# Decoder layer on one core: q and k transposed by DMA as fp16 halves, rotary sums on GpSimd, all engine orders laid out anew over eight stages

## What is computed

```python
x = x + attn(layernorm(x), wq, wk, wv, wo)      # causal, 8 heads of 128
x = x + xattn(layernorm(x), ctx, ctx)           # gelu(h @ ctx.T) @ ctx, 375 rows
x = x + ffn(layernorm(x), w1, b1, w2, b2)       # quantised to 8 bit, relu, 1024 hidden

# attn:
q, k = rope(rmsnorm(x @ wq)), rope(rmsnorm(x @ wk)); v = x @ wv
s = (q * mult) @ (k * mult).T - 1e30 * later
o = softmax(s) @ v;  return o @ wo
```

## Time and profile before

| | us |
|---|---|
| median of three runs | 731.2 (730.33 to 732.17) |
| the profiled execution | 730.79 |
| its span in the trace | 729.1 |
| one batch in the middle of the run | 21.39 |
| granted TensorE clock, mean | 0.986 |

### The profile page before, as it was taken

The page is one execution under the profiler, slowest core; times in us unless marked ns, Lnnn a source line. Parts: engine busy times, 40 slices in busy tenths (PEclk is TensorE's granted clock), DMA queues, the critical chain, the costliest instruction groups (busy, mean ns, idle before and its releaser), DMA issues.

```text
span 729.1 us, 15114 instructions
## 1 busy us (share of the span) xinstructions
PE 697.2 (96%) x5504; PEld 609.9 (84%) x5504; DVE 642.4 (88%) x1232; ACT 486.9 (67%) x1226; POOL 248.3 (34%) x393
## 2 busy tenths in 40 slices
PE   5599999999999999999999999999999999999974
PEld 4488888888888888888888989889888888888863
DVE  6989999999999999999999999999999999998942
ACT  5667766677766677776667767666777766677742
POOL 1344333433332343333234243333334333433310
PEclk9899999999999999999999999999999999999996
DMA  8501110111111011111111111101111110111100
GB/s 268 204 8 49 49 48 24 54 57 49 55 48 42 26 55 55 48 52 51 32 35 55 55 48 48 52 22 47 55 53 50 48 47 24 54 50 43 49 7 13
DMA packets 23946, 38.86 MB, mean 53 GB/s; under 512 B 2048, under 2 KB 18896, under 8 KB 23664
## 3 DMA queue, kind: packets, MB, share of 16 engines
q1 hardware_dynamic: 23920, 38.51, 17.5%
HBM read 34.84 MB, written 3.67 MB: 53 GB/s over the span
## 4 chain that ended last, share of the span: by engine, by line
PE 89%; DVE 3%; ACT 3%; issue 2%; DMA 2%; SPq 0%; POOL 0%; POOLq 0%; DVEq 0%; ACTq 0%
PE psum L846 34%; PE psum L833 17%; PE psum L874 7%; PE psum L854 6%; PE psum L911 6%; PE psum L920 6%; PE psum L945 4%; PE psum L937 3%; PE psum L881 3%; PE psum L902 2%; DMA w_raw<-in_wv 1%; DMA w_raw<-in_w 1%; ACT qkn L743 1%; PE psum L927 1%; DVE turn_c L492 0%
## 5 line engine op out<-in xcount | busy, mean ns | idle before, releaser
L846 PE MATMUL psum<-wqkv_hi,xnT_hi 128*112 128x512 f32 x384 | 165.1, 430 | 4.8 <-DVE wqkv_lo L433 2.8
L846 PE MATMUL psum<-wqkv_lo,xnT_hi 128*112 128x512 f32 x384 | 152.3, 397 | 0.0
L846 PE MATMUL psum<-wqkv_hi,xnT_lo 128*112 128x512 f32 x384 | 131.4, 396 | 0.0
L697 ACT ACTIVATE sq<-psum 112x1024 f32<-112x1024 f32 x64 | 65.5, 1023 | 79.7 <-PE psum L846 79.7
L344 POOL TENSOR_TENSOR rstd<-ve,nhalf 112x1 f32<-112x1 f32 x96 | 55.4, 578 | 156.0 <-DVE ve L407 151.0
L351 POOL TENSOR_TENSOR rms<-ms,nhalf 112x8 f32<-112x8 f32 x64 | 106.3, 1662 | 5.0
L733 ACT ACTIVATE w_raw<-psum,rden 112x128 f32<-112x128 f32 x256 | 69.5, 384 | 45.7 <-DVE rden L519 45.7
L846 PEld LDWEIGHTS psum<-wqkv_hi,xnT_lo 128*112 128x112 f32 x384 | 67.5, 176 | 22.1
L846 PEld LDWEIGHTS psum<-wqkv_hi,xnT_hi 128*112 128x112 f32 x384 | 68.1, 177 | 21.4 <-issue 3.1
L476 DVE TENSOR_TENSOR turn_c<-psum,cos_t 112x1024 f32<-112x1024 f32 x64 | 78.1, 1220 | 6.2 <-ACT sq L697 5.6
L468 DVE TENSOR_REDUCE ss<-sq 112x4 f32<-112x512 f32 (+1 forms) x95 | 81.9, 862 | 0.0
(11 more groups left out here) (82 smaller groups left out, 1531.4 us busy)
## 6 DMA issues: line engine op xcount, KB each, us to landing
ctx_in<-in_ctx_rows SPq DMA_DIRECT2D x32, 375.0 KB
ctxT<-in_ctx_cols SPq DMA_DIRECT2D x32, 375.0 KB, 6.4
x_in<-in_x SPq DMA_DIRECT2D x32, 112.0 KB, 2.0
out_y<-y_out SPq DMA_DIRECT2D x32, 112.0 KB, 1.9
w_raw<-in_w SPq DMA_DIRECT2D x2, 1024.0 KB, 7.5
w_raw<-in_wq SPq DMA_DIRECT2D x2, 512.0 KB, 4.6
w_raw<-in_wk SPq DMA_DIRECT2D x2, 512.0 KB, 6.3
w_raw<-in_wv SPq DMA_DIRECT2D x2, 512.0 KB, 8.0
```

The lines of the kernel that those rows point to most:

```text
L846: last = pe.matmul(ps[:, n, :], left[:, c, :], right[:, c, w, n * BANK:(n + 1) * BANK], start=c == 0 and left is xnT_hi and right is wqkv_ ...
```

## The change

- The scaled q and k no longer pass through PE. ACT writes their rounded fp16 halves straight from `turn_c` and `rms`, head by head, for q and now for k too (`round_q0/1`, `round_k0/1`, 16 instructions for a batch). DVE makes the low halves, also head by head (`split_q`, `split_k`, 16 instructions that read two SBUF operands and a pointer scalar). `qk16` holds both halves, 112 x 2048 fp16 for q and as much for k (448 KB each), and SP issues a transposing DMA for each into `qkT`. PE's 16 transposes, ACT's two rounding copies of 896 columns, DVE's two subtractions of 896 columns and `normalise_k` are gone.
- The rotary sums go from DVE to POOL (`turn_q`, `turn_k`).
- The loop is gone: all 39 bodies are written out, and each batch now spreads over eight stages (a to h) where it had five. x normalised and transposed in a; q, k and half of v projected in b; the other half of v, scores and weighting in c; the output projection in d; cross attention in e and f; the feed-forward part in f to h.
- The order of every engine and the PSUM banks of every product are new. `add_b2` now waits for `out_done` of the batch before, so it runs after `residual_out`. Waits that another wait already covers are left out.

What is the same: the projections, scores, weighting and all other products, in number and shape. In each projection the three products are now made one behind another for each half.

```diff
-            def turn(w, j):
-                dve.tensor_tensor(turn_c[:, w, :], turn_c[:, w, :], turn_s[:, w, :], ALU.add).then_inc(qk_turned[w], 1)
-            def normalise_k(j):
-                dve.tensor_tensor(heads(qkn[:, 1, :]), heads(turn_c[:, 1, :]),
-                                  rms[:, 1, :].unsqueeze(2).broadcast_to([T, H, D]), ALU.mult).then_inc(k_normed, 1)
-            def transpose_qk(w, j):
-                pe.wait_ge(qk_normed[w], done(j))
-                for h in range(H):
-                    last = pe.transpose((qT_ps, kT_ps)[w][:, h // HH, (h % HH) * T:(h % HH + 1) * T],
-                                        qkn[:, w, h * D:(h + 1) * D], ident[0:T, 0:T])
+            def transpose_q(j):
+                sp.wait_ge(q_lo_done, done(j))
+                sp.dma_start_transpose(qkT[:, 0], qk16[:, 0].rearrange("t l n -> t (l n)")).then_inc(qT_landed, 16)
+            def turn_q(j):
+                pool.wait_ge(q_cos_done, done(j))
+                pool.tensor_tensor(turn_c[:, 0, :], turn_c[:, 0, :], turn_s[:, 0, :], ALU.add).then_inc(q_turned, 1)
+            def add_b2(j):
+                if j.has(1):
+                    pool.wait_ge(out_done, done(j.plus(-1)))
+            def split_q(j):
+                dve.wait_ge(q_hi0_done, done(j))
+                for h in range(H):
+                    at = slice(h * D, (h + 1) * D)
+                    last = dve.scalar_tensor_tensor(out=qk16[:, 0, 1, at], in0=turn_c[:, 0, at], scalar=rms[:, 0, h:h + 1],
+                                                    in1=qk16[:, 0, 0, at], op0=ALU.mult, op1=ALU.subtract)
+            def round_q0(j):
+                for h in range(0 * HH, 1 * HH):
+                    last = act.activation(qk16[:, 0, 0, h * D:(h + 1) * D], turn_c[:, 0, h * D:(h + 1) * D],
+                                          ACT.Copy, scale=rms[:, 0, h:h + 1])
+            def scores(j):
+                pe.wait_ge(qT_landed, landed_once(j))
+                pe.wait_ge(kT_landed, landed_once(j))
...
-            iterations(dve, body)
+            for i in range(-5, B + 2):
+                body(i)
```

More of the change, by code:

```diff
@@ L97, in decoder_layer @@
     OH = BANK // VW
[L98 removed]
+    assert S == SC * SP and D == P and HH * T <= BANK and SP <= P and B % SLOTS == 0 and T % 16 == 0
     with ExitStack() as stack:
@@ L239, in decoder_layer @@
[L239 to L256 removed]
+        ident_b_done = sem("ident_b_done")
@@ new lines, in project_out @@
+            def project_out(heads, j, first, last):
+                if is_first(j):
+                    pe.wait_ge(wo_done, 3)
+                for h in heads:
+                    pe.matmul(y_ps, oT_hi[:, h, :], wo_hi[:, h, :], start=first and h == heads[0], stop=False)
+                    pe.matmul(y_ps, oT_hi[:, h, :], wo_lo[:, h, :], start=False, stop=False)
+                    product = pe.matmul(y_ps, oT_lo[:, h, :], wo_hi[:, h, :], start=False, stop=last and h == heads[-1])
+                return product
@@ new lines, in transpose_rows, with project_v0, out_units @@
+            def transpose_rows(dst, src):
+                for c in range(MC):
+                    last = pe.transpose(dst[:, c * T:(c + 1) * T], src[:, c * P:(c + 1) * P], ident[0:T, 0:T])
+                return last
+            pe.wait_ge(ident_in, 16)
+            def project_v0(j):
+                if j.has(2):
+                    pe.wait_ge(x2_done, done(j.plus(-2)))
+                project(2, 0, v0_ps, j).then_inc(v0_ready, 1)
+            def out_units(j):
+                if j.plus(5).inside(B):
+                    pe.wait_ge(v1_copied, done(j.plus(5)))
+                if j.off == B - 1:
+                    pe.wait_ge(f0_q_done, done(j))
+                for c in range(FC):
+                    last = pe.matmul(f2_ps, f_q[:, c, :], w2T[:, c, :], start=c == 0, stop=c == FC - 1)
+                last.then_inc(f2_ready, 1)
@@ new lines, in ctx_hidden @@
+            def ctx_hidden(j):
+                pe.wait_ge(ctxT_landed[j.off % SLOTS], landed(j))
+                if j.off == B - 1:
+                    pe.wait_ge(xn2T_copied, done(j))
+                for c in range(SC):
+                    for m in range(MC):
+                        last = pe.matmul(h_ps[:, c * T:(c + 1) * T], ctxT[:, j.off % 2, m, c * SP:(c + 1) * SP], xn2T[:, m, :],
+                                         start=m == 0, stop=m == MC - 1)
+                last.then_inc(h_ready, 1)
```

1150 lines of the change are left out of this document (563 added, 587 removed).

## The result

The changed kernel is slower: **873.65 us** (871.66 to 873.95 over four runs) against 731.17 (730.33 to 732.17), a ratio of 1.1942 [1.1919, 1.1966]. The forecast was 698 with a range of 683 to 740. The execution profiled took 873.48 us, with a span of 871.8.

What follows compares the result with a forecast made beforehand. PE was taken to bound the kernel; without its transposes a batch needs 19.85 us. 32 x 19.85 = 635.2, plus 10 for waits, 51 for ends and 1.7 outside the span, gives 698 us, range 683 to 740.

Steps and rivals of the forecast that it cites:

- the one on the transposing DMAs: SP's queue: each 448 KB transpose lands in 2.0 to 7.6 us, 4.5 taken; q's has 6.2 before the scores.
- 4.5 is hidden: Transposing DMA of q: landing in 4.5 us fits the 6.2 available; at 7.6 PE would wait 1.4 each batch.
- the 10 us allowed for waits: PE's pace: small waits of 0.35 us a batch over the 28 full ones, 10 us.
- the first rival: GpSimd's additions hold VectorE at the shared port and close the loop: pace 20.8 to 21.4, 721 us; chance 0.26.
- the pace that the sums described: Work per batch: TensorE 19.85 us and setting the pace, VectorE 17.6, ScalarE 15.4, GpSimd 12.3.
- The head-wise splits: VectorE: 16 added instructions of 128 columns at 0.20 to 0.32 us each, 0.23 taken, 3.7 us a batch.
- No transposes, 1.54 less on PE: TensorE: the 16 transposes go and nothing is added, 21.39 to 19.85 us a batch, 49.3 us at most.
- The loop that comes next: From invert_sums of one batch to the next through ACT, split_q and DVE: 19.2 us, 0.6 less than PE.
- The ends: Filling and draining outside the pace: 51 us, between 44.6 and 62; PE idle 34 us in filling, 15 at the end.
- 0.76 for faster: Whole kernel: chance 0.76 of being faster than before, 0.20 slower, 0.04 within 0.3%.
- The slower cases, 748 and 752: VectorE becomes the bound at 22 us a batch, 748, chance 0.12; transposing DMAs late, 752, chance 0.14, two thirds slower.

Runs made afterwards that it cites:

- the reordering: Changed kernel with x loaded two bodies earlier, plus VectorE's clips and quantisation moved between cosines and sines of k, normalisations and GpSimd's roots moved too; 730.25 us.
- The pair with one step moved: The best version, 717.0 us, and the same with the sines of k in front of the clips and quantisation on VectorE, 755.12 us.
- the kernel with the sines first: The best version with the sines of k moved in front of the clips and the quantisation on VectorE; 755.12 us.
- The best version: Changed kernel with x two bodies earlier, VectorE reordered, and SP issuing k's and q's transposes before context rows (one body later), store and x; 717.0 us.

## Why the prediction was wrong

**The step that failed** is the one on the transposing DMAs. It asked when `qkT` lands for the scores, and when q's transpose is issued behind k's. It didn't ask what is behind them: the load of x. Before, x had a whole body (21.7 us) from its issue to its use and landed in 2.0. Now it is issued in the body that uses it, waits in SP's order for `split_k` of that body, and has 448 + 375 + 112 KB in front of it. That closed a loop of its own through SP, x and VectorE, 8.4 + 17.5 us long, and no rival had it; the sum put this wait at nothing. `split_k` and the transpose could stay in front: with only the context rows and the store moved behind x, the 117 us were back (756.73). The prediction's "4.5 is hidden" was right for the transposes (4.9 at the median of both, 5.6 for q's alone with 6.2 to spare; PE waited for `qkT` in 4 of the 32 batches at most) and beside the point. By its own sum: 32 x (25.94 - 19.85) = 195 us more, less the 10 us allowed for waits, less 9 for ends of 871.8 - 32 x 25.94 = 42 instead of 51, is 176; and 698 + 176 = 874.

The Trainium skill ("DMA: Bandwidth & Descriptors", Queues, rings and completion order) says that each DMA engine consumes the descriptors of a queue's ring in order. The runs agree: 112 KB land 2.0 us after their issue at the front of the queue, 2.5 behind a transpose, 5.8 behind a transpose, 375 KB and 112 KB. The rule, had it been weighed for x and not for q alone, gives the step that was missed.

**Holding**, the first rival: the mechanism was right and its size too small. It was priced at 2.2 us for the clip and thought partly avoidable, for 721 us at 1.2 a batch. It was 3.2 us of VectorE a batch in four instructions, because the mask holds too, which the prediction didn't count though it stood in the order of before and after. Once x was early the same four means still came to 2.6 us a batch. Without them the mean pace went from 21.7 to 20.8, so 0.9 of the 2.6 reached the pace, 26 us in all (756.19 to 730.25; the reordering moves other steps as well, so this is the holding with the order). The rest turned into waiting: VectorE is idle for 58 of the 400 us in the middle, where it was for 26. The pair with one step moved gives 38 us for `turn_k` and the quantisation by themselves. The Trainium skill ("SBUF — State Buffer", SBUF: two separate sides) has the shared port as an exclusive lock for a whole instruction. These traces agree for GpSimd's 112x1024 additions: the clip beside `turn_q` took 2.48 us to its 2.35. They don't for GpSimd's powers over 8 columns: in the kernel with the sines first, 87 of VectorE's splits, with two SBUF inputs, began and ended inside such a power, and none took over 0.35 us.

**Terms that held.** The best version runs at the pace that the sums described, so they can be read off its window: VectorE 17.78 (forecast 17.6), ScalarE 15.24 (15.4), TensorE 20.07 (19.85), GpSimd 13.36 (12.3; its wide additions took 2.36 to 2.39 against 2.33, and the rest is one addition over 8 columns, held by VectorE to 1.30 us for 0.20). The head-wise splits stand (2.17 - 0.35) / 7 = 0.26 us apart, where 0.23 was taken from 0.20 to 0.32. "No transposes, 1.54 less on PE" came true to 0.2 us, and unrolling was rightly costed at nothing.

**The loop that comes next** was forecast at 19.2 us, 0.6 under PE. In the best version the pace is 20.4, with PE idle for 0.3, and the chain runs through VectorE at `split_q`, the squares, the cosines and the sines of k, then the scores, the weighting (L973), and ScalarE's roundings of the next q, behind which `split_q` starts again:

```profile
403.22 1.92 DVE qk L472 x7
...
407.08 1.13 DVE ss L491
408.20 1.13 DVE turn_c L391
...
410.10 1.14 DVE turn_s L399
...
411.38 0.23 PE psum L948
...
415.67 1.77 PE psum L973 x16
...
420.97 1.16 ACT qk L693 x4
422.13 1.18 ACT qk L699 x4
```

The scores wait there for the sines of k, because they are written into the PSUM region of the projected k. The prediction's loop went from `invert_sums` to `invert_sums` and didn't look at regions. The wait is read from the chain and the code. The run with the sines first did take it away (TensorE's waits for them at the scores fell from 29 to 3), but the quantisation was then held for longer than that, so no run shows what this loop costs.

**The ends** were put at 51 us, with 62 as the upper bound. The best version has 714.5 - 32 x 20.4 = 61.7. Its idle time of TensorE is what was forecast: 30.1 us in the first 60 and 4.4 in the next 60 (34 forecast), 14.0 in the last 55 (15 forecast). What was left out is that TensorE also works at less: the granted clock of the first 60 us, in half of which TensorE is idle, is 0.80 there as a mean over the levels of 2.4 and 1.2 GHz, and it was 0.94 before. The same shows in TensorE's busy time, which the prediction wanted near 648: it is 712.0 in the changed kernel, at a mean clock of 0.933, and 657.7 in the best version, at 0.974. With 20.4 and 61.7 the forecast would have been 32 x 20.4 + 61.7 + 1.7 = 716, the time of the best version. So about 18 us of the miss lie in the size of loop and ends; the other 157, from 716 to 873.65, went with the order on SP and VectorE.

**Chances.** 0.76 for faster rested on cases that all had x as before. The slower cases, 748 and 752, were each about an engine or a transfer that the change makes new work for; the one that came was about a transfer of the same size as before, in a new place.

## What to carry to other kernels

When a step is moved to a DMA queue, list what is queued behind it and give each item three times: when it can now be issued, when it lands with all that is queued before it, and when it is needed. A load takes over the dependence of whatever stands in front, and with a whole body to spare that costs nothing. Where the spare time is short, put the load in front of the bulk that nobody needs yet, or issue it bodies earlier. An instruction moved to GpSimd was free here where VectorE had products from PSUM or reductions beside it, so before moving one, write down which VectorE instruction stands beside each microsecond of it.

## What the runs showed of the hardware

- VectorE's `tensor_scalar` over 256 columns from SBUF is held for the rest of a GpSimd addition over 1024 columns (0.23 became 2.48 us, 0.41 became 2.48) and of a mask over 896 (0.41 became 1.23 beside 0.98). Products from PSUM and reductions over 1024 columns aren't: beside `turn_q` and the mask they took 1.21 us in the best version.
- A small GpSimd instruction is held in turn: one element took 1.05 us instead of 0.18. The product from PSUM beside which it starts doesn't do it alone: an addition over 8 columns beside the cosines of k, with the sines behind them, took 0.20 in all 32 batches of the same run. What stands behind the product here is a clip of the hidden units, a `tensor_scalar`, and GpSimd's instruction ends 0.04 us after that clip in all 26 batches in which it took longer. So in these rows a `tensor_scalar` that is next in VectorE's order holds GpSimd up to 1.1 us before its own record begins; why so early no run shows.

```profile
428.80 1.21 DVE L385 TENSOR_TENSOR turn_c<-psum,cos_t 112x1024 f32<-112x1024 f32 x1
429.19 1.05 POOL L298 TENSOR_TENSOR pool_cell<-pool_cell 1x1 f32<-1x1 f32 x1 [0.30 <-ACT w_raw L746]
429.93 0.27 DVE L527 TENSOR_SCALAR f_q<-f_int 128x448 bf16<-128x448 int16 x1
```

- GpSimd's powers over 8 columns take 1.66 us and don't hold the head-wise splits, which have two SBUF operands: these stay at 0.344 beside them. The splits don't hold the power either. In the kernel with the sines first the power of q takes 2.09 us in 26 batches, beside a clip and five splits; in the last batch, where the splits stand beside it and the clip is past, it takes 1.65. What makes the others longer is open: in the best version the same clip starts a little later within the power, which stays at 1.65.
- A transposing DMA of 448 KB from SBUF to SBUF lands 3.5 us after its issue at best and 8.2 at worst in the changed kernel, and keeps SP for 1.3 to 4.4 us, depending on what is queued in front; a plain one of the same size keeps it for 0.5.
